# Moving a small network and four gate columns within the last tile's second layer

## The reference

```python
x = x + L0(x)   # fc1 (512->2048), exact gelu, fc2 (2048->384) beside an expert's (2048->128), by sequence
x = x + L1(x)   # a 512x512 matrix by subject
x = x + L2(x)   # below
x = x + L3(x)   # a 512x512 matrix by category

def L2(x):
    ctx = causal_ema(x, tau_ctx)
    wg = sigmoid(concat([x, ctx]) @ Wg.T + bg)
    gated = x * wg
    h1 = gelu(x @ Wn1.T + bn1)                      # 512 -> 128, the small network
    mod = 0.5 + sigmoid(h1 @ Wn2.T + bn2)           # 128 -> 4
    traces = [causal_ema(gated * mod[d], tau[d]) for d in range(4)]
    temporal = sum(traces[d] * softmax(blend)[d] for d in range(4))
    gate = sigmoid(temporal @ Wtemp.T + btemp)
    soma = gelu(x @ Wsoma.T + bsoma)
    out = (soma * gate) @ Wout.T
    return layernorm(out) * gamma + beta
```

## Time and profile before

| | us |
|---|---|
| median of three runs | 1289.14 (1289.04 to 1289.81) |
| the profiled execution, its own time | 1290.09 |
| its span, first to last instruction | 1288.2 |
| TensorE (PE) busy | 1273.0, 99% |
| VectorE (DVE) busy | 1065.2, 83% |
| ScalarE (ACT) busy | 720.4, 56% |
| granted TensorE clock, mean | 0.997 of full speed |

### The profile page before, as it was taken

One profiled execution on the slowest core, in us unless ns is written; L12 is line 12 of the kernel. 1 busy time (PEld: TensorE's weight loads), 2 busy tenths in 40 slices (PEclk: granted clock), 3 DMA queues, 4 the chain that ended last, 5 costly groups with the idle time before them and its releaser, 6 DMA issues.

```text
span 1288.2 us, 17504 instructions
## 1 busy us (share of the span) xinstructions
PE 1273.0 (99%) x6109; PEld 1067.1 (83%) x6109; DVE 1065.2 (83%) x1682; ACT 720.4 (56%) x1369; POOL 78.9 (6%) x118
## 2 busy tenths in 40 slices
PE   8999999999999999999999999999999999999998
PEld 7788888888888888888887888778888888888877
DVE  7977777787786987777875699999999989998974
ACT  6577565776565875566864343543635353535344
POOL 0010000000000000000000111002100200020000
PEclk9999999999999999999999999989999999999999
DMA  8357554658744658645558898866456555654301
GB/s 291 102 170 236 185 179 131 221 164 266 217 167 151 230 179 264 208 148 171 198 187 273 303 327 327 329 254 220 173 220 238 211 182 208 249 201 160 131 17 66
DMA packets 114288, 262.63 MB, mean 204 GB/s; under 512 B 10345, under 2 KB 32873, under 8 KB 109081
## 3 DMA queue, kind: packets, MB, share of 16 engines
q1 hardware_dynamic: 94336, 183.27, 41.5%
q10 hardware_dynamic: 15032, 62.45, 13.9%
q0 software_dynamic: 4832, 15.79, 3.2%
HBM read 181.19 MB, written 80.28 MB: 203 GB/s over the span
## 4 chain that ended last, share of the span: by engine, by line
PE 86%; DVE 8%; DMA 3%; ACT 1%; issue 1%; ACTq 0%; DVEq 0%
PE bank L1593 29%; PE bank L1595 28%; PE bank L1594 28%; DVE drive L2304 2%; DMA x_slot<-x2hl_dram 1%; DVE drive L2293 1%; DVE temporal L2315 1%; DVE t_lo L2059 0%; DMA x_raw<-in_x 0%; DMA hb_in<-hb_dram 0%; DVE spikes_lo L2059 0%; DVE x_raw L2211 0%; DVE w_hl L2059 0%; DMA mod_t<-mod_dram 0%; PE bank L1901 0%
## 5 line engine op out<-in xcount | busy, mean ns | idle before, releaser
L1593 PE MATMUL bank<-h_hl,w_hl 128*128 128x512 f32 x512 | 199.5, 390 | 0.1
L1594 PE MATMUL bank<-h_hl,w_hl 128*128 128x512 f32 x512 | 199.3, 389 | 0.0
L1595 PE MATMUL bank<-h_hl,w_hl 128*128 128x512 f32 x512 | 199.2, 389 | 0.0
L1593 PE MATMUL bank<-t_hi,sp_hl 128*128 128x512 f32 x448 | 175.2, 391 | 4.4 <-DVE t_lo L2059 1.9
L1594 PE MATMUL bank<-t_lo,sp_hl 128*128 128x512 f32 x448 | 174.4, 389 | 0.0
L1595 PE MATMUL bank<-t_hi,sp_hl 128*128 128x512 f32 x448 | 174.4, 389 | 0.0
L1593 PEld LDWEIGHTS bank<-h_hl,w_hl 128*128 128x128 f32 x512 | 96.1, 188 | 20.8 <-issue 1.1
L1595 PEld LDWEIGHTS bank<-h_hl,w_hl 128*128 128x128 f32 x512 | 96.1, 188 | 20.0
L1594 PEld LDWEIGHTS bank<-h_hl,w_hl 128*128 128x128 f32 x512 | 96.1, 188 | 19.9
L1593 PEld LDWEIGHTS bank<-t_hi,sp_hl 128*128 128x128 f32 x448 | 84.1, 188 | 25.0 <-issue 1.8
L1595 PEld LDWEIGHTS bank<-t_hi,sp_hl 128*128 128x128 f32 x448 | 84.1, 188 | 17.6
(11 more groups left out here) (228 smaller groups left out, 3037.0 us busy)
## 6 DMA issues: line engine op xcount, KB each, us to landing
wg_hl<-wg_dram ACTq DMA_DIRECT2D x24, 1536.0 KB, 7.4
fc_raw<-in_fc_w SPq DMA_DIRECT2D x32, 512.0 KB, 4.2
hb_dram<-hb_out SPq DMA_DIRECT2D x64, 256.0 KB, 2.3
hb_in<-hb_dram ACTq DMA_DIRECT2D x64, 256.0 KB, 4.1
x2hl_dram<-x_hl POOLq DMA_DIRECT2D x28, 512.0 KB, 5.7
x_slot<-x2hl_dram SPq DMA_DIRECT2D x26, 512.0 KB, 5.1
wg_hl<-wg_dram SPq DMA_DIRECT2D x8, 1536.0 KB, 8.2
stage<-in_l_w SPq DMA_DIRECT2D x32, 256.0 KB, 3.4
```

The costliest lines, as they stand in the source:

```text
L1593: eng.matmul(ps, w_hi, x_hi, start=first, stop=False, skip_group_check=resumed)
L1594: eng.matmul(ps, w_hi, x_lo, start=False, stop=False, skip_group_check=resumed)
L1595: return eng.matmul(ps, w_lo, x_hi, start=False, stop=final, skip_group_check=resumed)
```

## The change

On all engines the order of the seam is written anew; no instruction is added or removed, apart from waits.

- TensorE: `n1(0)` goes ahead of use 16 of tile 6, `mo(0)` ahead of use 1 of tile 7. Both now write bank 3, and use 1 waits for `s_mod` before it writes that bank. The gates stand behind uses 3, 5, 7 and 9 (before: 5, 8, 10, 12), two quarters of tile 6's `l1` each behind gate 0 and behind use 4 (before one each behind uses 3 to 6). Uses 10 to 16 follow each other with nothing between (before: 13 to 16).
- ScalarE: `h1_of` with use 2, `mod_of` ahead of use 3's copies; `q_of` and `wg_tanh` move up; the last `wg_tanh(0, 3)` is now in the seam.
- VectorE: `traces` of columns 0 to 2 stand 2 to 3 uses earlier and closer together.
- SP: `load_wg(0)`, the four `load_ctx(0, ·)` and both `load_xt(0, ·)` no longer wait for uses 1, 2 and 3, but stand behind the last products; the other loads move by one to three uses.
- GpSimd: the four `store_hl` of tile 6 lose their waits for uses and follow `last_columns(0, 0)`.

```diff
+                if p == PAIRS - 1:
+                    load_wg(0)
+                    for c in range(KC):
+                        load_ctx(0, c)
                 store_hb(p, K8 - 1, 0)
...
+            load_xt(0, 0)
+            load_xt(0, 1)
             uses_done(1)
-            load_wg(0)
             pass_staged(PAIRS - 1, K8 + 2)
             uses_done(2)
-            for c in range(KC):
-                load_ctx(0, c)
+            store_ctx(LAST - 2, 1)
+            load_wg(1)
             uses_done(3)
-            load_xt(0, 0)
-            load_xt(0, 1)
-            store_ctx(LAST - 2, 1)
+            load_wsoma(0)
+            load_wg(2)
...
+            last_columns(0, 0)
+            for c in range(KC):
+                store_hl(LAST - 1, c)
...
                 for v in range(13, HC):
+                    if p == PAIRS - 1 and v == HC - 1:
+                        n1(0)
                     fc2(2 * HC * p + v)
...
+                mo(0)
                 for j in range(HC):
                     fc2(2 * HC * p + HC + j)
-                    if j == 2:
-                        n1(0)
-                    if j == 3:
-                        mo(0)
-                    if j in (2, 3, 4, 5):
-                        l1(LAST - 1, j - 2)
-                    if j in (4, 7, 9, 11):
-                        gate(0, (4, 7, 9, 11).index(j))
+                    if j in (2, 4, 6, 8):
+                        gate(0, j // 2 - 1)
+                    if j in (2, 3):
+                        l1(LAST - 1, 2 * j - 4)
+                        l1(LAST - 1, 2 * j - 3)
```

More of the change, by code:

```diff
@@ L988, in _ @@
             modulation_back(0)
-            last_columns(0, 0, range(2))
-            store_last_hl(0)
-            last_columns(0, 0, range(2, TAUS))
-            last_columns(0, 1, range(2))
-            store_last_hl(1)
-            last_columns(0, 1, range(2, 3))
-            store_last_hl(2)
-            last_columns(0, 1, range(3, TAUS))
-            store_last_hl(3)
-            for c in range(HALVES, KC):
+            last_columns(0, 0)
+            for c in range(KC):
+                store_hl(LAST - 1, c)
+            for c in range(1, KC):
                 last_columns(0, c)
@@ L1425, in _ @@
                         load_hb(p, j + 1)
+                    if p == PAIRS - 1 and j == 2:
+                        mod_of(0)
                     if p == PAIRS - 1 or j < HC - 1:
@@ L1428, in _ @@
                         w2_hi(v)
+                    if p == PAIRS - 1 and j == 1:
+                        h1_of(0)
                     staged_hi(p, K8 + j)
@@ L1440, in _ @@
                         continue
-                    if j == 4:
-                        h1_of(0)
+                    if j in (5, 7, 9, 11):
+                        q_of(0, (j - 5) // 2)
                     if j == 5:
-                        mod_of(0)
-                    if j in (7, 10, 12):
-                        q_of(0, (7, 10, 12).index(j))
+                        wg_tanh(0, 0)
                     if j == 7:
-                        wg_tanh(0, 0)
-                    if j == 11:
+                        for c in range(KC):
+                            x2_hi(t, c)
                         wg_tanh(0, 1)
-                    if j == 14:
+                    if j == 10:
                         wg_tanh(0, 2)
-                        q_of(0, 3)
+                    if j == 12:
                         ctx_hi(t, 0)
                         ctx_hi(t, 1)
-                    if j == 15:
+                    if j == 13:
+                        wg_tanh(0, 3)
+                    if j == 14:
                         ctx_hi(t, 2)
                         ctx_hi(t, 3)
-            wg_tanh(0, 3)
             for c in range(KC):
@@ L1693, in fc2 @@
                         on.wait_ge(s_x2, KC * (t - 1) + m + 1)
+                    if at == 0 and t == LAST and m == KC - 1:
+                        on.wait_ge(s_mod, 1)
                     mm = split_product(acc_of_tile(t)[m][:, :], w2_hl[v % 3][:, 0, m, :], w2_hl[v % 3][:, 1, m, :],
@@ L1720, in n1 @@
                     on.wait_ge(s_soma, KC * (i - 1) + 2)
[L1721 to L1724 removed]
+                elif i:
+                    on.wait_ge(s_x1, KC * LAST)
+                    on.wait_ge(s_gated, 3)
+                else:
+                    on.wait_ge(s_hlo, use_of_c21(PAIRS - 1, K8 - 1) + 1)
                 on.wait_ge(s_wn1, 16)
@@ L1762, in gate @@
                         on.wait_ge(s_soma, 1)
-                    else:
-                        on.wait_ge(s_mod, 1)
                 elif m == 1:
@@ L2571, in _ @@
                         continue
-                    if j in (5, 6, 7, 8):
-                        x2_of(t, j - 5)
-                    if j == 7:
+                    if j == 5:
                         gate_sum(0, 0)
                         traces_a(0, 0)
+                        x2_of(t, 0)
+                        x2_of(t, 1)
+                        traces_b(0, 0)
+                    if j == 6:
+                        x2_of(t, 2)
+                        traces_c(0, 0)
+                        x2_of(t, 3)
+                        traces_d(0, 0)
@@ L2577, in _ @@
+                    if j == 7:
+                        for c in range(KC):
+                            x2_lo(t, c)
+                        gate_sum(0, 1)
+                        traces_a(0, 1)
                     if j == 8:
-                        traces_b(0, 0)
+                        traces_b(0, 1)
+                        context(t, 0)
                     if j == 9:
-                        x2_lo(t, 0)
-                        x2_lo(t, 1)
-                        traces_c(0, 0)
+                        traces_c(0, 1)
+                        traces_d(0, 1)
+                        context(t, 1)
@@ L2583, in _ @@
                     if j == 10:
-                        x2_lo(t, 2)
-                        x2_lo(t, 3)
-                        traces_d(0, 0)
-                        gate_sum(0, 1)
+                        gate_sum(0, 2)
+                        traces_a(0, 2)
+                        context(t, 2)
                     if j == 11:
-                        traces_a(0, 1)
-                        traces_b(0, 1)
+                        traces_b(0, 2)
+                        context(t, 3)
                     if j == 12:
-                        traces_c(0, 1)
@@ L2593, in _ @@
-                        gate_sum(0, 2)
-                        context(t, 0)
-                        context(t, 1)
-                    if j == 14:
-                        traces_d(0, 1)
-                        context(t, 2)
-                        context(t, 3)
-                    if j == 15:
+                        gate_sum(0, 3)
                         context_lo(t, 0)
                         context_lo(t, 1)
-                        traces_a(0, 2)
-            context_lo(LAST - 1, 2)
```

48 lines of the change are left out of this document (18 added, 30 removed).

## The result

| | kernel before | changed kernel |
|---|---|---|
| median of the runs beside each other | 1289.92 us (6 runs) | 1294.45 us (6 runs) |
| ratio | | 1.0039, 95% interval 1.0028 to 1.0051 |
| profiled execution, its span | 1290.09, 1288.2 us | 1293.45, 1291.5 us |

A forecast was written before the change was run, and what follows sets the result against it. TensorE was taken as the bound, busy 1273.0 of 1288.2 us, with only a 4.2 us wait to win; 710.8 - 707.1 + 1.0 = 4.7, less 0.35, net +4.3 on 1289.14: 1293.4 us, range 1289.2 to 1297.5.

The forecast's parts named there:

- the forecast 0.35: Behind the seam: earlier ctx stores let the load of n1(1)'s slot go sooner, a gain of 0.35 us.
- The lead: VectorE behind the seam: 7.5 us of work done ahead, none of it reaching line 1901; value 0.
- T: Moment when traces_a(0, 0) ends on VectorE: forecast 710.8 (708.0 to 715.7); the seam ends later by T - 707.1.
- La: Time of use 4's hb_in load on ScalarE's queue, in SP's crowd of loads: 7.2 us (6.3 to 8.5).
- Lb: Time of use 6's hb_in load, in a tie with ctx_dram, wg(1), wsoma(0): 5 us, between 2.6 and 8.5.
- rival B: Loads of hb_in are in time: T = 708.0, loss 0.55 us, 1289.7, no change; chance 0.22.
- the list from T to use 13: VectorE's work from T to the low parts of use 13: 44.8 us in sum.
- use 10's load: Load issued at 728.2 beside bunched x2hl stores and wg(3), 0.8 us late: costs 1.0 us (0 to 2.5).
- its own signs: Wrong if line 1901's wait is gone, VectorE stands idle before use 13, or T is before 709.
- Rival A: The forecast itself: VectorE's list is late at use 13; 1293.4, with 1290.7 to 1296; chance 0.58.
- C: Clock falls in the new wait of 3.5 to 4 us before use 13: 1296.0; chance 0.14.
- D: VectorE's 7.5 us of lead do reach line 1901: -7 + 4.3, 1286.4, faster; chance 0.06.

The follow-up runs named there:

- ctx_late: wg4_late with VectorE's context scans of columns 2 and 3 moved behind the low parts of uses 14 and 15; 1293.72 us, one run.
- both_late: Changed kernel with traces b and c of column 2 put back behind the seam and wg(4) put back behind use 13; 1289.83 us, ratio 1.0003.
- lead_free: both_late with traces_b(0, 2) moved on VectorE ahead of x1_of, into a hole of 4 us; 1289.75 us, ratio 1.0004.
- loads_only: Kernel before with only the changed kernel's order of loads and stores on SP and GpSimd; 1293.51 us, ratio 1.0033.
- traces_late: Changed kernel with traces_b(0, 2) and traces_c(0, 2) put back behind the seam on VectorE; 1291.40 us, ratio 1.0018.
- loads_paced: Kernel before with only SP's changed order; GpSimd's four hi-lo stores of x2 keep their waits for uses; 1290.37 us, ratio 1.0008.
- wg4_late: Changed kernel with the load wg(4) put back behind use 13 on SP, instead of behind use 10; 1294.29 us, ratio 1.0040.
- slots_first: sumsq_early with the loads of l3w(0) put behind the slots of tile 2 on SP; 1289.77 us, ratio 1.0004.
- sumsq_early: Kernel before with sum_squares(0) swapped ahead of first_traces(1, 2) on VectorE; 1291.23 us, ratio 1.0012.

## Why the prediction was right

**The place and the size.** Uses 13 and 15 wait for low parts of VectorE, 3.25 and 0.50 us where 3.5 to 4 and 0.6 were forecast. For the seam 4.7 us were forecast, and so(0, 0) is 4.05 us late; for the whole 4.3, and the span is 4.06 longer (3.3 and the 0.76): from so(0, 0) to gate(1, 0) the forecast 0.35 came back (22.80 us for 23.18), and behind the sum of squares 0.4 were lost again, whose cause stays open. The medians have 1.0039, some 5.0 us (3.6 to 6.6). ctx_late and both_late show the mechanism.

**The lead.** Value 0, for the reason given: items of VectorE's list that wait for TensorE, and one that waits for ScalarE. lead_free shows it by itself.

**T, the step that failed.** La was forecast as 7.2 us and Lb as 5; they were 7.2 (690.08 to 697.27) and 5.0 (697.53 to 702.55). Between them I had put four copies, 2.2 us. ScalarE in order of time has the next load 0.23 us behind the start of the first copy:

```profile
697.30 0.63 ACT L1101 ACTIVATE h_hl<-hb_in 128x512 fp32r<-128x512 f32 x1 [1.18 <-DMA hb_in<-hb_dram]
697.53 0.33 ACTq L1097 DMA_DIRECT2D hb_in<-hb_dram  x1
697.83 0.62 ACT L1034 ACTIVATE w_hl<-w_raw 128x512 fp32r<-128x512 f32 x1
```

So T was 708.0 where 710.05 was forecast in this trace's time, close to its lower end: of the loss, the late loads of uses 4 and 6 carry only some 0.7 us, and on this step rival B (708.0, for 708.7 measured in the time of the kernel before and 710.8 forecast) was nearer. What made up for it is the list from T to use 13. It took 47.2 us (707.96 to 755.12), not 44.8 plus 1.0 for use 10's load: VectorE stood idle 0.51, 0.62, 0.43 and 0.42 us in it, the last of these for use 10. The two errors, 2.0 too late and 1.4 too short, cancel for the most part. The number was better than its working, and that is luck. By its own signs the prediction was in part wrong: T is before 709, and VectorE stood idle before use 13, two of the three things that it named. The third, a wait at line 1901 that is gone, did not come.

**A bound that doesn't follow.** Rival A's upper end, 1296, is not what its own terms give: with T at 715.7 the sum is 1289.14 + 8.6 + 1.0 - 0.35 = 1298.4, above the range as well. The measured time doesn't touch it.

**What was not seen.** wg(4) leaving together with use 14's load, a second cause of 1.7 us in the shadow of the first; and the order of loads and stores by itself, which costs the kernel before some 4 us (loads_only) though the changed kernel nothing but that 1.7 (both_late). Had VectorE's list been in time, I would have forecast no change, and the load of use 14 would have made it 0.18% slower (traces_late).

**The rivals.** B rested on the two queues taking turns, and the prediction says that the trace disagrees. That was read too quickly: they do take turns, by packets, and it doesn't help the small load (last section). C: the clock stayed up in the new wait of 3.1 us. Windows of the changed kernel (busy times, then the granted clock, DMA share, GB/s) for uses 12 and 13, and for the stretch of the earlier trace rows:

```profile
750.00:756.00 6.00, 2.92 (x13) 2.12 (x12) 5.93 (x10) 1.67 (x4) 1.74 (x2) 1.00 0.84 325
834.00:850.00 16.00, 11.75 (x41) 8.54 (x40) 15.62 (x20) 6.77 (x12) 0.00 (x0) 0.79 0.83 301
```

D was priced at 7 us, and that was wrong as well: squares that come 2.3 us earlier with respect to TensorE gave nothing, and with slot and holes mended too the gain can't be told from 0. The wait of 0.24 us on n1(1)'s slot is gone, as forecast. The modulation, the fourth column of use 1 and the 36 matmuls of a gate cost nothing.

## What to carry over

A wait that is the largest in the list need not be a bound worth anything: take half of it away in an experiment and see which wait grows, before you price what would reach it. Where one semaphore releases a small load that is due soon and a large one that is not, put the large one behind another step: once both are under way they take turns by packets, and a small load of as many packets is through no sooner than the large one. And an order that gives an in-order engine a lead pays only if what stands behind it has no anchor in another engine's order.

## What the hardware did that was not expected

**Two queues, one order.** A load of 256 KB on ScalarE's queue took 2.6 to 2.9 us when it was issued 0.2 to 0.9 us ahead of SP's 1536 KB, and 7.1 to 8.7 us when issued 0.1 to 0.4 us behind it (six traces: loads_paced, both_late, traces_late; loads_only, wg4_late and the changed kernel). Issued in the same hundredth of a microsecond it took 7.5 and 7.8, as long as the large one. The count of packets says why. ScalarE's queue is q10: while the load for use 14 was alone in wg4_late (747.36 to 750.10) it moved 128 packets of 2 KB and 16 of under 512 B:

```profile
q10 hardware_dynamic: 144, 0.26, 32.0%
```

SP's 1536 KB are 128 packets as well, of 12 KB. With both under way (traces_late, 750.5 to 751.5; packets, MB, share of the engines) the queues moved the same number of packets, at six times the bytes for SP's, q1:

```profile
q1 hardware_dynamic: 30, 0.37, 87.1%
q10 hardware_dynamic: 29, 0.06, 15.2%
```

So they took turns packet by packet, and the small load, with as many packets, was through with the large one. And the later it was issued, the more of the large one had gone ahead before its own first packet (windows of half a microsecond): some 15 packets when issued together (traces_late), 30 to 40 at 0.09 us behind (loads_only), 90 at 0.29 (changed kernel), 100 at 0.92 (kernel before). Issued 0.18 us ahead (traces_late, use 3) it had moved some 125 packets when the large one had moved 9. The Trainium skill ("DMA: Bandwidth & Descriptors", "Queues, rings and completion order") has each DMA engine go round-robin between the queues, a packet at a time. Where both queues had packets under way these traces agree; what doesn't follow is that the small load lands first. Whether fewer and larger packets for it would help was not tested.

**A transfer overtakes the copies ahead of it.** In the changed kernel ScalarE issued the load for use 6 at 697.53, 0.23 us after the copy of use 4's block began, and the load for use 7 at 700.75, 0.07 us after that of use 5's, while other copies that stand ahead of it in program order were still to run (at 697.83 above, and at 701.22).

**The clock and a wait.** A wait of 3.1 us between uses left the clock at full speed. At the sum of squares 4.2 us brought it to half, and 1.9 us did in one kernel and not in the other. The windows of slots_first, then of sumsq_early:

```profile
830.00:845.00 15.00, 13.10 (x49) 10.06 (x48) 14.54 (x19) 5.94 (x12) 0.00 (x0) 0.89 0.74 232
```

```profile
830.00:845.00 15.00, 12.27 (x52) 9.20 (x50) 14.58 (x18) 5.89 (x12) 0.00 (x0) 1.00 0.75 272
```

Both waited 1.9 us at the same matmul. So the length of a wait alone doesn't decide it; what does was not settled here.
